# Key and value projections of the first attention as four matmuls at 32-column positions

## Chip, cores, metric

One of the cores of a Trainium2 chip runs the whole kernel. The metric is the device time of one execution in microseconds (us); a lower time is better. Times given "by the profile" are those of one profiled execution.

## What is computed

`x` holds 1024 tokens of 128 features, `ctx_768` 6404 context tokens of 96 features. Four layers follow each other, each an attention of `x` over the context and a feed-forward part, each behind a layer norm and with a residual:

```python
x = x + _L0_xattn_ref(_layernorm(x), ctx_768, ...)   # 16 heads of 8
x = x + _L0_ffn_ref(_layernorm(x), ...)              # 8 experts, top 2
x = x + _L1_xattn_ref(_layernorm(x), ctx_768, ...)   # 16 heads of 64
x = x + _L1_ffn_ref(_layernorm(x), ...)              # fp8 product
x = x + _L2_xattn_ref(_layernorm(x), ctx_768, ...)   # 16 heads of 8
...                                                  # layer 2 experts, layer 3
```

What the change touches belongs to the second attention, `_L1_xattn_ref`, but is worked on inside the first:

```python
k = (context @ Wk).reshape(B, Nk, h, dh)     # Wk, Wv: 96 x 1024, h = 16, dh = 64
v = (context @ Wv).reshape(B, Nk, h, dh)
```

## The kernel before

The program is written by engine, with semaphores set by hand. In the first attention (`attention8(0, 0)`, 16 heads of 8) the heads stand in 4 groups of 4, and each group is worked on for two halves of 512 tokens: 8 passes. A pass goes over the context in 51 tiles (ST) of 128 tokens. For each tile TensorE makes

- the scores, `qk` (L442): four matmuls, each with 32 rows of the array for one head (32 by 128), 512 moving columns, fp32r;
- the attention values, `av` (L454): four matmuls, each with all 128 rows and 32 columns of the array (128 by 32), that write 32 partitions each of one PSUM bank and accumulate over the tiles, fp32.

ScalarE turns the scores into exponentials (L999, two per tile, 128 by 1024), GpSimd stages the tile's keys and values (L1249, L1250). The scores of a tile are issued ahead of the attention values of the tile before it. Scores have six banks, so they wait until an exponential has read the banks that they write.

In between TensorE makes the keys and values of the second attention, since their weights don't depend on `x`. A pass serves one pair of its heads (128 features): `projections1` makes 13 chunks (NC) of up to 512 context tokens for the keys and 13 for the values, 26 jobs (JOBS), the last chunk of each with 384 tokens. JOB_STEPS spreads the jobs over the tiles: in a pass 26 of the 51 tiles have one, between the scores of the next tile and the attention values of this one. All 8 passes together have 208 jobs. A key job (L427) is one matmul with the weights `w[0]` as stationary operand and 512 context columns moving; a value job (L430) is four matmuls (three in the last chunk), each with 128 context tokens as stationary and the 128 columns of `w[1]` moving. Both use the whole 128 by 128 array and write one bank, `ps[:, 7 - half, :]`, which VectorE copies out (L1555, in `move1`) after the semaphore `kv_proj`; a DMA of SyncE's queue then stores the copy to DRAM (L2106). `kv_moved` tells TensorE that the bank is free for the next job. Which of two branches runs is read from data; in this run it is `straight`, in which the tiles are written out one by one. The branch `group`, which also calls `projections1`, is not run.

The two weight matrices `w64` have 128 rows; those beyond the 96 features are part of the contraction as they are, and the change leaves that alone. A matmul of fp32 goes through the array in two passes, and the profile records each with its own weight load: a key job has 2 records of MATMUL and 2 of LDWEIGHTS, a value job 8 and 8, `av` 8 and 8, `qk` (fp32r) 4 and 4.

Of the kernel before, what the change touches and what calls it, by code (L numbers as in the profile page):

```python
# [13 lines left out]
P = 128  # L14
# [20 lines left out]
G = 4  # L35
# [52 lines left out]
def build_program(nc, a):  # L88

    ctx = ExitStack()  # L90
    with ctx:
        def sb(name, shape, dt=F32):
            return ctx.enter_context(nc.sbuf_tensor(name, shape, dt))
# [11 lines left out]
        ctxT = sb("ctxT", [P, NC * HT])  # L105
# [92 lines left out]
        def tok(ap, t):  # L198

            return ap[:, t // 4, (t % 4) * P:(t % 4 + 1) * P]  # L200
# [31 lines left out]
        def _(pe):  # L232
# [93 lines left out]
            for t in range(NT):  # L326
                mm = pe.transpose(ps[:, t // 4, (t % 4) * P:(t % 4 + 1) * P], xn[:, t, :], ident[:, :])
            mm.then_inc(s["turned"], 1)
            for g, (t0, n) in enumerate(VG):
# [6 lines left out]
                for u in range(n):  # L336
                    mm = pe.transpose(ps[0:C, 2 + g % 4, u * P:(u + 1) * P], cn[:, t0 + u, :], ident[:, :])
# [63 lines left out]
            def attention8(n, layer):  # L401
                w = w8[:, n]
# [12 lines left out]
                def projections1(g, half, jobs):  # L415

                    w = [w64[:, 2 * half + m, :] for m in range(2)]
                    bank = ps[:, 7 - half, :]
                    for m, c in jobs:
                        c0, wd = CHUNKS[c]  # L420
                        if m == 0 and c == 0:
                            pe.wait_ge(s["in_wkv"], g * 64 + 32 * half + 32)
                            if half or g is not first_group:
                                pe.wait_ge(s["den_copied"], g * 2 + half + DENS[0])
                        pe.wait_ge(s["kv_moved"], (g * 2 + half) * JOBS + m * NC + c + 1)
                        if m == 0:
                            mm = pe.matmul(bank[:, 0:wd], w[0], ctxT[:, c0:c0 + wd], start=True, stop=True)  # L427
                        else:
                            for u in range(0, wd, P):
                                mm = pe.matmul(bank[:, u:u + P], ctxT[:, c0 + u:c0 + u + P], w[1], start=True, stop=True)  # L430
                        mm.then_inc(s["kv_proj"], 1)

                def queries_ready(g, half):
# [24 lines left out]
                def group(gi, par):  # L458
                    g = gi if n == 0 else gi * 2 + par
                    for half in range(2):  # L460
                        def qk_maxima():
                            queries_ready(g, half)
                            for j in range(G):
                                band = slice(32 * j, 32 * j + 32)
                                mm = pe.matmul(ps[:, j, :], kst[band, 0, :], qh[band, half, :], start=True, stop=True)
                            return mm

                        maxima(layer, g * 2 + half, G, 2 * ST, qk_maxima)
                        def last_sums():
                            if half:  # L470
                                denominators(g * 2, 0)
                            elif n == 0:
                                if g is not first_group:
                                    denominators(g * 2 - 1, 1)
                            elif par:
                                denominators(gi * 4 + 1, 1)
                            else:
                                with pe.If(gi >= 1):
                                    denominators(3, 1)

                        first = (g * 2 + half) * ST + TILES[layer]
                        if n == 0:
                            stream_jobs(first, lambda t, r: qk(half, t, r), lambda *at: av(g, half, *at), last_sums,
                                        lambda step: projections1(g, half, [(step // JSTEPS, c) for c in JOBS_AT[step % JSTEPS]]))
                        else:
                            stream(first, lambda t, r: qk(half, t, r), lambda *at: av(g, half, *at), last_sums)

                def straight():

                    queries_ready(0, 0)  # L490
                    qk(0, TILES[layer], 0)
                    for gh in range(2 * NG):
                        g, half = gh // 2, gh % 2
                        for t in range(ST):
                            at = gh * ST + t + TILES[layer]
                            if t + 1 < ST:
                                qk(half, at + 1, (t + 1) % RING)
                            elif gh + 1 < 2 * NG:
                                queries_ready((gh + 1) // 2, 1 - half)
                                qk(1 - half, at + 1, 0)  # L500
                            if n == 0:
                                projections1(g, half, [divmod(k, NC) for k in range(JOBS) if JOB_STEPS[k] == t - RING])
                            av(g, half, at, t % RING, t == 0, t + 1 == ST)
                            if t == RING - 1 and gh:
                                denominators(gh - 1, 1 - half)
# [16 lines left out]
                for half in range(2):  # L522
                    for g in range(NG):
                        if g == NG - 1:
                            pe.wait_ge(s["o_done"], SUMS[layer] + 2 * g + half + 3)
                        mm = pe.matmul(ps[:, 4 + half, :], w[:, 3 + g, :], sums[:, 2 * g + half, :],
                                       start=(g == 0), stop=(g == NG - 1))
# [58 lines left out]
            for h in range(2):  # L586
                mm = pe.matmul(ps[:, h, :], wT[:, 0, :], z[:, h, :], start=True, stop=True)
            mm.then_inc(s["p_proj"], 1)
            pe.wait_ge(s["p_ready"], 1)
            for t in range(NT):  # L590
                pe.matmul(ps[:, 6, t * E16:t * E16 + E8], tok(t1, t), wT[:, 5, 0:E8], start=True, stop=True)
                mm = pe.matmul(ps[:, 6, t * E16 + E8:t * E16 + E8 + 1], tok(t2, t), ones[:, 0:1], start=True, stop=True)
# [8 lines left out]
            for p in range(NP):  # L601
                cut = slice(p * P, (p + 1) * P)
                mm = pe.matmul(ps[:, 6 + p // 4, (p % 4) * P:(p % 4 + 1) * P], wqk1[0:C, 0, cut], wqk1[0:C, 0, cut],
                               start=True, stop=True)
# [19 lines left out]
            for p in range(NP):  # L624
                if p >= 2:
                    pe.wait_ge(s["b1_copied"], p - 1)
                for h in range(2):
                    mm = pe.matmul(ps[:, 2 * (p % 2) + h, :], wqk1[:, 1, p * P:(p + 1) * P], z[:, h, :], start=True, stop=True)
# [107 lines left out]
            for p in range(NP):  # L736
# [4 lines left out]
                for h in range(2):  # L741
                    mm = pe.matmul(ps[:, h, :], wo8[:, p, :], qo[:, p, h, :], start=(p == 0), stop=(p == last_pair))
# [23 lines left out]
            for t in range(NT):  # L766
                mm = pe.matmul(ps[:, 6, t * E16:t * E16 + E8], tok(z, t), wr2[:, :], start=True, stop=True)
# [3 lines left out]
            for t in range(NT):  # L771
                mm = pe.matmul(ps[:, t // 4, (t % 4) * P:(t % 4 + 1) * P],
                               stat[:, 16 + t:17 + t].to_broadcast([P, P]), ident[:, :], start=True, stop=True)
# [4 lines left out]
            for t in range(ST):  # L778
                k = P if t < SF else TAIL
                mm = pe.matmul(ps[0:C, 2, 0:C], cn2[0:k, t, :], cn2[0:k, t, :], start=(t == 0), stop=(t == ST - 1))  # L780
# [6 lines left out]
            for h in range(2):  # L787
                mm = pe.matmul(ps[:, h, :], wT[:, 1, :], z[:, h, :], start=True, stop=True)
# [3 lines left out]
            for h in range(2):  # L792
                mm = pe.matmul(ps[:, 2 + h, :], wk3[:, :], t1[:, h, :], start=True, stop=True)
# [4 lines left out]
            for h in range(2):  # L798
                mm = pe.matmul(ps[:, 4 + h, :], stat[:, 0:1].to_broadcast([P, P]), z[:, h, :], start=True, stop=True)
# [3 lines left out]
            for g, (t0, m) in enumerate(VG):  # L803
                if g >= 2:
                    pe.wait_ge(s["v3_copied"], g - 1)
                for u in range(m):
                    mm = pe.matmul(ps[:, 6 + g % 2, u * P:(u + 1) * P], ctxT[0:C, (t0 + u) * P:(t0 + u + 1) * P],
                                   wT[0:C, 3, :], start=True, stop=True)
# [22 lines left out]
            for h in range(2):  # L831
                mm = pe.matmul(ps[:, h, :], ones_b[:, :], t2b[:, h, :], start=True, stop=True)
# [8 lines left out]
            for t in range(NT):  # L841
                mm = pe.matmul(ps[:, 0, t:t + 1], tok(t3, t), ones[:, 0:1], start=True, stop=True)
            mm.then_inc(s["den_ready"], 1)
            pe.wait_ge(s["rec_ready"], SUMS[3] + 1)
            for t in range(NT):
                mm = pe.matmul(tok(ps[:, 2:4, :], t), ccol[:, 1, t:t + 1].to_broadcast([P, P]), ident[:, :], start=True, stop=True)
            mm.then_inc(s["den8"], 1)
            pe.wait_ge(s["o_done"], SUMS[3] + 3)
            for h in range(2):
                mm = pe.matmul(ps[:, 2 + h, :], wT[:, 2, :], t1[:, h, :], start=True, stop=True)  # L850
# [5 lines left out]
            for t in range(NT):  # L856
                mm = pe.matmul(ps[:, 6, t * E16:(t + 1) * E16], tok(z, t), wT[:, 4, 0:E16], start=True, stop=True)
# [54 lines left out]
            for t in range(NT):  # L912
                mm = pe.transpose(ps[0:E16, 6 + t // 4, (t % 4) * P:(t % 4 + 1) * P], route[:, 7, t * E16:(t + 1) * E16], ident[:, :])
# [13 lines left out]
            for t in range(NT):  # L927
                mm = pe.transpose(ps[:, t // 4, (t % 4) * P:(t % 4 + 1) * P], tok(xT, t), ident[:, :])
# [1291 lines left out]
```

## Time and profile before

| | us |
|---|---|
| median of 3 runs | 4024.19 |
| their lowest and highest | 4022.65 to 4025.73 |
| profiled execution, its own time | 4020.67 |
| its span, first to last instruction | 4018.9 |
| first attention's eight passes, by the trace | 80.6 to 955.3 |
| TensorE busy | 3690.8 (92% of the span) |
| ScalarE busy | 2595.9 (65%) |
| VectorE busy | 1716.9 (43%) |
| mean granted TensorE clock | 0.979 |

The profile records each engine's instructions with start and modelled or measured end. PE stands for the matmuls, PEld for the weight loads, which can lie beside matmuls; DVE is VectorE, ACT ScalarE, POOL GpSimd, SP SyncE. Matmuls are pipelined, so a record's length is more than the time until the next can start: prices of matmuls are read from start to start. An engine's idle time is put down to what released it.

### The profile page before, as it was taken

How to read it: one execution, taken by the hardware profiler on the slowest of the kernel's cores; microseconds unless marked ns; L12 is line 12 of the kernel's file. 1: busy time of each engine (PE TensorE's matmuls, PEld its weight loads, DVE VectorE, ACT ScalarE, POOL GpSimd, SP SyncE). 2: the span in 40 equal slices, each digit the busy share in tenths (PEclk: the TensorE clock that was granted, in tenths of full speed). 3: DMA queues.
4: the chain of work that ended last, by engine and by line, in shares of the span. 5: the costliest groups of instructions: out<-in, count | busy, mean ns of one | idle time of the engine just before them, and what ended most of it. 6: DMA issues, size and time to landing. Idle time of an engine off the chain costs nothing.

```text
span 4018.9 us, 75707 instructions
## 1 busy us (share of the span) xinstructions
PE 3690.8 (92%) x26700; PEld 1367.5 (34%) x26704; DVE 1716.9 (43%) x1661; ACT 2595.9 (65%) x2756; POOL 464.7 (12%) x1844
## 2 busy tenths in 40 slices
PE   7999999998989999999999999968888888798989
PEld 4333333334533333333333333331111111355444
DVE  4212222223167777777777777640000000443344
ACT  5888888885345555555655555459999999202321
POOL 1222222221000000000000000002222222100210
PEclk8999999999989999999999999989999999899989
DMA  5223222211211111111111110050101000100000
GB/s 175 87 77 92 74 83 81 89 62 45 83 40 38 41 38 37 42 38 36 43 36 38 41 38 5 6 155 3 37 3 37 4 3 1 41 26 1 0 10 29
DMA packets 109842, 182.57 MB, mean 45 GB/s; under 512 B 23700, under 2 KB 46896, under 8 KB 107408
## 3 DMA queue, kind: packets, MB, share of 16 engines
q1 hardware_dynamic: 109584, 178.75, 14.4%
q8 instruction: 209, 3.42, 0.3%
q14 instruction: 49, 0.40, 0.0%
HBM read 107.13 MB, written 71.57 MB: 44 GB/s over the span
## 4 chain that ended last, share of the span: by engine, by line
PE 70%; ACT 15%; issue 10%; DVE 4%; ACTq 1%; SPq 0%; DMA 0%; POOLq 0%; DVEq 0%; POOL 0%
PE ps L657 18%; PE ps L682 17%; ACT probs L999 14%; PE ps L454 6%; PE ps L442 5%; PE ps L561 3%; PE ps L430 3%; PE ps L427 3%; PE ps L540 2%; PE ps L815 2%; PE ps L826 2%; PE ps L874 2%; PE ps L888 1%; PE ps L547 1%; PE ps L256 1%
## 5 line engine op out<-in xcount | busy, mean ns | idle before, releaser
L999 ACT ACTIVATE probs<-ps 128x1024 f32<-128x1024 f32 x1632 | 1520.1, 1085 | 137.2 <-PE ps L442 137.1
L1096 ACT ACTIVATE probs<-ps 128x1024 f32<-128x1024 f32 x816 | 835.8, 1024 | 595.0 <-PE ps L657 580.6
L1728 DVE TENSOR_TENSOR vbuf<-vbuf,probs 128x1024 f32<-128x1024 f32 (+1 forms) x800 | 972.5, 1224 | 333.5 <-ACT probs L1096 333.5
L454 PE MATMUL ps<-probs,vst 128*32 128x512 f32 x6528 | 872.8, 607 | 137.3 <-ACT probs L999 137.0
L442 PE MATMUL ps<-qz,kst 32*128 32x512 f32 x3264 | 415.2, 494 | 57.0 <-ACT probs L999 38.5
L442 PEld LDWEIGHTS ps<-qz,kst 32*128 32x128 f32 x3264 | 167.1, 182 | 748.1 <-issue 555.2
L1555 DVE COPY qs<-ps 128x512 f32<-128x512 f32 (+1 forms) x208 | 141.7, 681 | 647.6 <-PE ps L430 339.3
L1249 POOL CAST kst<-kb 128x128 fp32r x816 | 240.9, 295 | 1373.8 <-PE ps L454 1263.7
L657 PE MATMUL ps<-probs,kb 64*64 64x512 f32 x2560 | 332.3, 589 | 0.0
L1594 DVE COPY work<-ps 128x512 f32 x16 | 11.1, 692 | 702.6 <-PE ps L454 702.6
L657 PE MATMUL ps<-probs,qz 64*64 64x512 f32 x2048 | 268.2, 594 | 6.7 <-issue 6.4
L454 PEld LDWEIGHTS ps<-probs,vst 128*32 128x32 f32 x6528 | 129.1, 108 | 407.7 <-ACT probs L999 328.5
L682 PE MATMUL ps<-probs,qz 64*64 64x512 f32 x2048 | 267.1, 592 | 0.0
L682 PE MATMUL ps<-probs,kb 64*64 64x512 f32 x2048 | 265.8, 589 | 0.0
L1250 POOL COPY vst<-vbuf 128x36 f32 x816 | 177.8, 218 | 0.0
L657 PEld LDWEIGHTS ps<-probs,kb 64*64 64x64 f32 x2560 | 97.9, 133 | 176.7 <-issue 176.7
L1275 POOL COPY probs<-kb 128x512 f32<-128x512 f32 x16 | 14.8, 934 | 1135.3 <-PE ps L657 1080.0
L1017 ACT ACTIVATE probs<-ps,stat 128x1024 f32<-128x1024 f32 x51 | 56.8, 1113 | 123.0 <-PE ps L815 123.0
L682 PE MATMUL ps<-probs,klo 64*64 64x512 f32 x1024 | 132.9, 589 | 0.0
L657 PE MATMUL ps<-probs,klo 64*64 64x512 f32 x1024 | 132.9, 589 | 0.0
L682 PE MATMUL ps<-probs,qs 64*64 64x512 f32 x1024 | 132.9, 589 | 0.0
L540 PE MATMUL ps<-work,vbuf 128*128 128x512 f32 x256 | 121.3, 623 | 9.5 <-DVE probs L1615 8.0
(364 smaller groups left out, 3037.1 us busy)
## 6 DMA issues: line engine op xcount, KB each, us to landing
kv_scratch<-qs SPq DMA_DIRECT2D x192, 256.0 KB, 2.0
kb<-k_scratch SPq DMA_DIRECT2D x24, 816.0 KB, 7.1
kb<-kv_scratch SPq DMA_DIRECT2D x72, 256.0 KB, 2.8
qz<-kv_scratch SPq DMA_DIRECT2D x64, 256.0 KB, 2.9
k_scratch<-klo SPq DMA_DIRECT2D x24, 512.0 KB, 3.3
vbuf<-in_L_ffn_W SPq DMA_DIRECT2D x32, 256.0 KB, 3.1
klo<-kv_scratch SPq DMA_DIRECT2D x32, 256.0 KB, 2.9
qs<-kv_scratch SPq DMA_DIRECT2D x24, 256.0 KB, 3.0
```

Of the source, the lines that this page charges most:

```text
L427: mm = pe.matmul(bank[:, 0:wd], w[0], ctxT[:, c0:c0 + wd], start=True, stop=True)
L442: mm = pe.matmul(ps[:, (4 * r + j) % (2 * RING), :], kst[band, r, :], qh[band, half, :], start=True, stop=True)
L454: mm = pe.matmul(ps[32 * j:32 * j + 32, 6 + half, :], vst[:, r, 32 * j:32 * j + 32], probs[:, r, j * HT:(j + 1) * HT], start=start, stop=stop)
L540: mm = pe.matmul(ps[:, 2 * (f % 2) + h, :], wts[:, f * P:(f + 1) * P], z[:, h, :], start=True, stop=True)
L657: mm = pe.matmul(ps[key, 2 * b + e, :], kk[t // 4][head, (t % 4) * P + HD64 * kh:(t % 4) * P + HD64 * (kh + 1)], qp[head, odd, h, :], star ...
L682: mm = pe.matmul(ps[head, 4 + 2 * h + kh, :], vv[t // 4][key, (t % 4) * P + HD64 * e:(t % 4) * P + HD64 * (e + 1)], pr1[key, (i + 2 * odd) ...
L999: act.activation(probs[:, r, b * T:(b + 1) * T].rearrange("p (h n) -> p h n", h=2), ps[:, 2 * buf:2 * buf + 2, :], ACT.Exp, scale=HD8 ** - ...
L1096: act.activation(pr1[:, (u + 2 * odd) % 4], ps[:, 2 * b:2 * b + 2, :], ACT.Exp, scale=HD64 ** -0.5)\
L1249: pool.tensor_copy(kst[:, r, :], kb[:, par, bass.ds(t * P, P)]).then_inc(s["staged"], 1)
L1250: pool.tensor_copy(vst[:, r, :].rearrange("p (j w) -> p j w", j=G)[:, :, 0:HD8 + 1], vbuf[:, bass.ds(t * (H * (HD8 + 1)) + g * (G * (HD8 + ...
L1555: dve.tensor_copy(kvst[:, slot, 0:wd], ps[:, 7 - half, 0:wd]).then_inc(s["kv_moved"], 1)
L1728: dve.tensor_tensor(sum1[0:k, odd, h], sum1[0:k, odd, h], e, ALU.add).then_inc(s["added"], 1)
```

## The change

Both branches of `projections1` issue each matmul as four, one for each 32 columns of the stationary operand. Matmul `j` writes partitions `32 j` to `32 j + 31` of the same bank: for the keys these are 32 output features of `w[0]`, for the values 32 context tokens. The moving operand is the same for the four. Waits, the semaphore increment on the last matmul, banks and the other engines' programs stay.

```diff
                         if m == 0:
-                            mm = pe.matmul(bank[:, 0:wd], w[0], ctxT[:, c0:c0 + wd], start=True, stop=True)
+                            for j in range(G):
+                                cut = slice(32 * j, 32 * j + 32)
+                                mm = pe.matmul(bank[cut, 0:wd], w[0][:, cut], ctxT[:, c0:c0 + wd], start=True, stop=True)
                         else:
                             for u in range(0, wd, P):
-                                mm = pe.matmul(bank[:, u:u + P], ctxT[:, c0 + u:c0 + u + P], w[1], start=True, stop=True)
+                                for j in range(G):
+                                    cut = slice(32 * j, 32 * j + 32)
+                                    mm = pe.matmul(bank[cut, u:u + P], ctxT[:, c0 + u + 32 * j:c0 + u + 32 * j + 32], w[1],
+                                                   start=True, stop=True)
                         mm.then_inc(s["kv_proj"], 1)
```

## Rows read from the trace of the kernel before

**Rows 1.** The page: busy time of each engine, then the chain that ended last.

```profile
PE 3690.8 (92%) x26700; PEld 1367.5 (34%) x26704; DVE 1716.9 (43%) x1661; ACT 2595.9 (65%) x2756; POOL 464.7 (12%) x1844
...
PE 70%; ACT 15%; issue 10%; DVE 4%; ACTq 1%; SPq 0%; DMA 0%; POOLq 0%; DVEq 0%; POOL 0%
PE ps L657 18%; PE ps L682 17%; ACT probs L999 14%; PE ps L454 6%; PE ps L442 5%; PE ps L561 3%; PE ps L430 3%; PE ps L427 3%; PE ps L540 2%; PE ps L815 2%; PE ps L826 2%; PE ps L874 2%; PE ps L888 1%; PE ps L547 1%; PE ps L256 1%
```

**Rows 2.** Table by stage: two passes of layer 0, one of layer 2; header names columns.

```profile
core 0: us, PE busy (x) PEld busy (x) DVE busy (x) ACT busy (x) POOL busy (x), PEclk, DMA share, GB/s
189.70:299.10 109.40, 103.34 (x742) 34.99 (x742) 23.06 (x30) 96.36 (x103) 23.54 (x102) 1.00 0.22 75
299.10:408.50 109.40, 103.33 (x742) 35.00 (x742) 23.06 (x30) 96.35 (x103) 23.41 (x102) 1.00 0.35 89
...
2774.00:2869.00 95.00, 78.55 (x618) 18.80 (x618) 5.91 (x5) 94.19 (x104) 23.75 (x104) 1.00 0.02 4
```

**Rows 3.** The chain that ended last, 605.72 to 609.95: start us, us, what.

```profile
605.72 0.49 PE ps L442 x4
606.21 1.01 ACT probs L999
607.22 0.14 issue
607.35 0.51 PE ps L442 x4
607.86 1.09 PE ps L430 x8
608.95 0.99 PE ps L454 x8
```

**Rows 4.** Groups by line, six passes, 190 to 846 us: busy, mean ns | idle before.

```profile
L999 ACT ACTIVATE probs<-ps 128x1024 f32<-128x1024 f32 x613 | 579.1, 1031 | 78.3 <-PE ps L442 78.3
...
L1555 DVE COPY qs<-ps 128x512 f32<-128x512 f32 (+1 forms) x156 | 106.3, 681 | 469.9 <-PE ps L430 254.4 <-PE ps L427 215.5
```

**Rows 5.** Timeline of TensorE around one key job: start us, us, what.

```profile
311.28 0.51 PE L442 MATMUL ps<-qz,kst 32*128 32x512 f32 x4
311.71 0.70 PE L427 MATMUL ps<-ctxT,w 128*128 128x512 f32 x1
312.25 0.59 PE L427 MATMUL ps<-ctxT,w 128*128 128x512 f32 x1
312.77 0.64 PE L454 MATMUL ps<-probs,vst 128*32 128x512 f32 x4
313.22 0.61 PE L454 MATMUL ps<-probs,vst 128*32 128x512 f32 x4
313.76 0.50 PE L442 MATMUL ps<-qz,kst 32*128 32x512 f32 x4
```

**Rows 6.** Timeline of TensorE around one value job and the tile after it.

```profile
603.56 0.38 PE L430 MATMUL ps<-w,ctxT 128*128 128x128 f32 x1
...
604.22 0.50 PE L430 MATMUL ps<-w,ctxT 128*128 128x128 f32 x3
604.34 0.39 PE L430 MATMUL ps<-w,ctxT 128*128 128x128 f32 x2
604.65 0.64 PE L454 MATMUL ps<-probs,vst 128*32 128x512 f32 x4
...
605.65 0.51 PE L442 MATMUL ps<-qz,kst 32*128 32x512 f32 x4
606.09 0.64 PE L454 MATMUL ps<-probs,vst 128*32 128x512 f32 x4
```

**Rows 7.** Timeline of the weight loads in the same stretch.

```profile
603.56 0.97 PEld L430 LDWEIGHTS ps<-w,ctxT 128*128 128x128 f32 x8 [0.25 <-issue]
604.65 0.16 PEld L454 LDWEIGHTS ps<-probs,vst 128*32 128x32 f32 x8
```

**Rows 8.** Timeline, second attention: matmuls of one shape in a row, and loads.

```profile
1700.25 1.04 PE L682 MATMUL ps<-probs,work 64*64 64x512 f32 x8
1701.11 1.04 PE L657 MATMUL ps<-probs,qz 64*64 64x512 f32 x8
...
1700.68 0.15 PEld L657 LDWEIGHTS ps<-probs,qz 64*64 64x64 f32 x4 [0.28 <-issue]
```

**Rows 9.** Weight loads of L427, then of L454: ns min/median/max, starts, forms.

```profile
L427 PEld LDWEIGHTS ps<-ctxT,w x208: 186/188/190, 86.9 to 899.8; 128*128 128x128 f32 x104
...
L454 PEld LDWEIGHTS ps<-probs,vst x6528: 105/108/153, 80.7 to 3433.8; 128*32 128x32 f32 x198
```

**Rows 10.** The page: instructions in all, and the queue that fetches them.

```profile
span 4018.9 us, 75707 instructions
...
q8 instruction: 209, 3.42, 0.3%
```

## Prediction, made before the changed kernel had run

> **What bounds the kernel now.** I read the page first [rows 1]: TensorE (PE) is busy for 92% of the span and carries 70% of the chain that ended last, so time taken off PE can be time taken off the end, if it is taken where PE leads. The two edited lines are L427 (key projection) and L430 (value projection), each 3% of that chain. They run only in the eight head-group passes of the first attention, 80.6 to 955.3 us. The table by stage [rows 2] shows what leads there: a pass takes 109.4 us, ScalarE is busy for 96.4 of them, PE for 103.3, and the granted clock is 1.00. The same attention in layer 2, without projections, takes about 95 us per pass with ScalarE busy for almost all of it. So ScalarE sets a floor near 95 to 96, and the projections put some 14 us on top of it in each pass.
>
> The chain of waits in one stretch [rows 3] shows how. Where a tile carries a projection, the chain goes scores (L442), projection, attention values (L454), scores, and only then to an exponential; the whole 1.09 us of the projection stands in it. The lines over six passes [rows 4] say the same from ScalarE's side: it sits idle for 78.3 us before its exponentials, all of it waiting for L442. Six passes hold 156 projection jobs (26 each: 13 chunks, for keys and for values), so each job makes ScalarE wait some 0.50 us. Anything up to that which a job gives back goes straight to the end of the pass; above it ScalarE would hold the pace. VectorE only copies each result out [rows 4], 0.68 us of work in a pass-step of over 2 us, and waits for PE before it.
>
> **The change part by part.** It touches no wait, no semaphore, no DMA and no other engine. One 128x128 stationary load and one matmul become four loads of 32 columns and four matmuls, each writing 32 partitions, with the same moving columns. Every matmul here goes through the array in two passes (the records count two per matmul), so a value job of four token blocks goes from 8 load-and-matmul pairs to 32, a key job from 2 to 8.
>
> First the prices, in the stretch of one key job [rows 5]. From scores to the projection, 311.28 to 311.71, is 0.43 us, and from scores straight to attention values [rows 6], 605.65 to 606.09, is 0.44: leaving the scores' shape costs the same whichever shape follows, so this entry stays. Inside the key job the first pass lasts 0.54 (311.71 to 312.25) although 512 columns stream in 0.43, which the steady stream of L657 and L682 shows (four passes at a time, 0.86 for two [rows 8]). The extra 0.11 is the first load of 128 columns, which nothing hides. The attention values pay the same thing for 32 columns only: 312.77 to 313.22 is 0.45, an extra of 0.02 to 0.03. The load records agree [rows 9]: 188 ns for 128 columns, 108 for 32, a difference of 0.08. The second pass of the key job is followed after 0.52 (312.25 to 312.77), again 0.09 over the 0.43. Attention values to scores shows it too: 313.22 to 313.76 is 0.54, which is 0.43, some 0.02 for the stagger of the four, and 0.09. L657 to L682, which share a shape, shows none of it [rows 8]. So 0.09 is the price of changing the array's shape when full-height (128-row) work is in it, and the edit removes one such change per job, because projection and attention values then have the same shape.
>
> A key job after the edit: 0.03 for the first loads, 0.43 and 0.43 for two rounds of four, 0.89 against 1.06 now. Its attention values then find their first weights loaded behind it, 0.97 against 0.99 to 1.00. Together 0.195 less.
>
> A value job [rows 6]: now 603.56 to 604.65, 1.09, with a pitch of 0.11 between passes of 128 columns (604.22 to 604.34). After: 0.03 and eight rounds at 0.11, 0.91, if four column positions stream at once and the next block's loads hide behind them as they do now. With 0.02 to 0.03 off the attention values, 0.20 less. Eight of the 104 jobs of each kind are shorter ones (384 columns), with the same extras saved.
>
> Sum: 104 x 0.195 + 104 x 0.20 = 41 us. All of it is on the chain, since it is less than the 0.50 that ScalarE waits per job; next late after it is still this wait, at 0.30.
>
> **Unknown costs.** The trace has no column-tiled matmul of 128 moving columns, none whose four positions stream the same columns, and no such density of instructions. The bounds for the value job: below, loads and streaming perfectly overlapped, 0.88 (gain 0.03 more per job, 3 us in all). Above, the four positions run one after another: 32 pairs at the present pitch of 0.11, 3.5 us. I take 0.91, because the nearest row by shape, L454, starts all eight of its loads within a record of 0.16 us while L430's eight take 0.97 [rows 7], and its four matmuls share each round. In [rows 8] the loads of the next group start right behind the last round of the group before on the same positions. Sharing the same moving columns can't gain anything; I price it at zero, with the serial case as its other end. Instruction fetch: a key job gains 6 matmul records, a value job 24 (18 where it is short), and as many loads, some 6,100 records on top of 75,707 [rows 10]. A pass then has about 1,130 matmul records instead of 742 [rows 2], 1.5 times the rate. The instruction queue moves 209 packets for the whole, 362 records to a packet on average, and each takes 0.3% x 16 x 4018.9 / 209 = 0.9 us. No row of now shows PE waiting for one, so I price it at zero; its other end is that every packet of the eight passes shows, (11,860 + 6,140) / 362 = 50 of them, 45 us.
>
> Against the change stands a rule of the Trainium skill, page TensorE: Matmul & The Clock Gate, section Back-to-back issue gap: a stream of weight load and matmul pairs at 128 moving columns was seen to sustain about 81 ns per pair. Taken as a limit for the whole engine, an estimate from that page makes the value job 32 x 0.081 = 2.6 us and the kernel 104 x (2.6 - 1.09) - 20 = 137 us slower. It is the mechanism of the first rival below, which has its price from rows. The eight pairs of L454 in [rows 7] start in far less, but they are a burst and not a stream, so the trace doesn't refute it.
>
> The page TensorEngine Tiling (Array Packing), section Key Properties, says that changing the tiling mode drains the engine; rows show the 0.09, but also that leaving the 32-row scores costs nothing, which the page doesn't distinguish. By the page alone the number of changes falls from three to two a job as well.
>
> **Rivals.** *Pairs are issued too slowly (slower).* Four times as many pairs pass through one sequencer and one queue. The streaming of a value job needs a new pair every 0.11 / 4 = 28 ns. If a pair costs p, the job takes 32p; a value job is worse than now above 1.09 / 32 = 34 ns, and above some 40 ns, (1.09 + 0.20) / 32, it also eats the keys' 20 us. The densest sustained stream in the trace is eight pairs in 0.86 us [rows 8], 107 ns each, and it is paced by its columns, so it bounds nothing tighter; at that price the job takes 3.4 us, 2.35 more, and the kernel 104 x 2.35 - 20 = 224 us slower, 4248. At twice the needed 28 ns it would be 1.8 us, +0.7 each, 53 us slower, 4077. For it: nothing so dense is in the trace. Against: the bursts of [rows 7].
>
> *Values gain nothing, keys do.* The reordering across four positions doesn't reach over to the next token block: each block of 128 columns then pays its first loads and a stagger, 0.05 to 0.08 four times, and the value job ends where it was. Then only the keys' 20 us are left, 4004. Against it: [rows 8].
>
> *The edit doesn't save the change of shape.* The 0.09 might belong to the wait of L454 rather than to the shape. Then 0.08 and 0.02 per job stay, 21 us, 4003. Against: the same 0.09 stands before L442 as well.
>
> *No change.* The saved time is given back by instruction fetch, up to the 45 us above: about 4024.
>
> **How the numbers follow.** The profiled execution took 4020.67 us (span 4018.9); less 41 is 3979.7. The median of the three timed runs, 4024.19, lies 3.5 above it, and less 41 it is 3983. Chances: forecast 0.72 (3977 to 3992); values gain nothing, or the shape change stays, together 0.14 (near 4003); no change 0.05; slower by the issue of pairs 0.09. The range is 3976 to 4005: the forecast, its lower bound of 3 us more with the spread of the runs, and the partial cases, 0.86 together. A measurement of this kernel can tell about 0.2%, 8 us, from no change. Faster 0.86, same 0.05, slower 0.09.
>
> **What would show it.** Right: a pass of 104.2 us instead of 109.4; L454 following the last round of L427 after 0.43, not 0.52; key jobs of 0.89 and value jobs of 0.91 from first start to L454's first; ScalarE's idle before L999 down from 0.50 to 0.30 per job; later stages unchanged. Wrong: value rounds pitched wider than 0.11, loads of L430 that don't start in fours, or gaps in PE at regular numbers of instructions.

## The result

The changed kernel takes 3980.13 us, median of four runs (3977.84 to 3985.2), against 4023.9 for the kernel before, median of four (4022.65 to 4025.73). The ratio is 0.9893, 95% interval 0.9875 to 0.991: 1.1% faster, clear of the 0.2% that can be told from no change. The forecast was 3983. Measured again beside the last of the experiments it took 3982.65 (four runs), ratio 0.9903 (0.9886 to 0.9919).

The page of the changed kernel, and its table by stage for two passes (these rows answer to [rows 1], [rows 2] and [rows 10]; L429 is now the key projection, L434 the value projection, L459 the attention values, L447 the scores, L1004 the exponentials):

```profile
span 3978.8 us, 81851 instructions
PE 3650.2 (92%) x29772; PEld 1357.5 (34%) x29776; DVE 1716.5 (43%) x1661; ACT 2596.5 (65%) x2756; POOL 465.9 (12%) x1844
...
q8 instruction: 233, 3.82, 0.4%
```

```profile
core 0: us, PE busy (x) PEld busy (x) DVE busy (x) ACT busy (x) POOL busy (x), PEclk, DMA share, GB/s
184.20:288.20 104.00, 98.01 (x1130) 33.29 (x1130) 23.03 (x30) 96.32 (x103) 23.70 (x102) 1.00 0.24 80
288.20:392.20 104.00, 98.03 (x1130) 33.32 (x1130) 23.05 (x30) 96.34 (x103) 23.59 (x102) 1.00 0.36 94
```

A pass went from 109.4 to 104.0 us at the same granted clock of 1.00. The whole execution has 6,144 more records and 24 more packets of instructions, 256 records for each packet gained. ScalarE's work in a pass is the same, 96.3; what shrank is its wait. Groups by line of the changed kernel, the same six passes (184.2 to 808.8 us), as in [rows 4]:

```profile
L1004 ACT ACTIVATE probs<-ps 128x1024 f32<-128x1024 f32 x613 | 579.1, 1031 | 46.5 <-PE ps L447 45.5
```

ScalarE's wait for the scores was 78.3 us and is 46.5: 0.30 us for each of the 156 jobs instead of 0.50, as forecast. The timeline of TensorE in the changed kernel, first around a key job (as [rows 5]), then around a value job (as [rows 6] and [rows 7]), columns start us, us, what:

```profile
511.73 0.51 PE L447 MATMUL ps<-qz,kst 32*128 32x512 f32 x4
512.16 0.64 PE L429 MATMUL ps<-ctxT,w 128*32 128x512 f32 x4
512.62 0.61 PE L429 MATMUL ps<-ctxT,w 128*32 128x512 f32 x4
513.05 0.61 PE L459 MATMUL ps<-probs,vst 128*32 128x512 f32 x4
513.48 0.61 PE L459 MATMUL ps<-probs,vst 128*32 128x512 f32 x4
514.02 0.51 PE L447 MATMUL ps<-qz,kst 32*128 32x512 f32 x4
```

```profile
452.05 0.32 PE L434 MATMUL ps<-w,ctxT 128*32 128x128 f32 x4
...
452.62 0.51 PE L434 MATMUL ps<-w,ctxT 128*32 128x128 f32 x12
452.73 0.40 PE L434 MATMUL ps<-w,ctxT 128*32 128x128 f32 x8
452.94 0.61 PE L459 MATMUL ps<-probs,vst 128*32 128x512 f32 x4
453.92 0.51 PE L447 MATMUL ps<-qz,kst 32*128 32x512 f32 x4
...
452.05 0.81 PEld L434 LDWEIGHTS ps<-w,ctxT 128*32 128x32 f32 x32 [0.25 <-issue]
452.84 0.24 PEld L459 LDWEIGHTS ps<-probs,vst 128*32 128x32 f32 x8
```

Read from start to start: the key job is 513.05 - 512.16 = 0.89 (1.06 before), the value job 452.94 - 452.05 = 0.89 (1.09), the attention values 514.02 - 513.05 = 0.97 (0.99). The second round of the key job is followed by L459 after 0.43, not 0.52. The first loads of L459 begin at 452.84, 0.10 before its first matmul: they run while the value job's last round still streams. In [rows 7] the first load of L454 begins only with its matmul, at 604.65. Over all full-size jobs of the trace the medians are 0.882 for keys (1.056 before), 0.897 for values (1.088) and 0.972 behind either (0.996).

### The profile page after: what moved, and what is told of

Read it like the earlier page. It is cut to its first block, busy times and chain, and to the rows that moved or that the text cites. A ratio compares the mean times of both kernels' runs of the same rounds, so it can differ in the third digit from the quotient of the medians.

```text
span 3978.8 us, 81851 instructions
## 1 busy us (share of the span) xinstructions
PE 3650.2 (92%) x29772; PEld 1357.5 (34%) x29776; DVE 1716.5 (43%) x1661; ACT 2596.5 (65%) x2756; POOL 465.9 (12%) x1844
## 4 chain that ended last, share of the span: by engine, by line
PE 69%; ACT 15%; issue 10%; DVE 4%; ACTq 1%; SPq 0%; DMA 0%; POOLq 0%; DVEq 0%; POOL 0%
PE ps L662 18%; PE ps L687 18%; ACT probs L1004 14%; PE ps L459 5%; PE ps L447 5%; PE ps L566 3%; PE ps L434 3%; PE ps L429 3%; PE ps L820 2%; PE ps L545 2%; PE ps L831 2%; PE ps L879 2%; PE ps L893 1%; PE ps L552 1%; PE ps L256 1%
## 5 line engine op out<-in xcount | busy, mean ns | idle before, releaser
L1004 ACT ACTIVATE probs<-ps 128x1024 f32<-128x1024 f32 x1632 | 1520.1, 1085 | 93.9 <-PE ps L447 92.4
L459 PE MATMUL ps<-probs,vst 128*32 128x512 f32 x6528 | 867.0, 603 | 139.3 <-ACT probs L1004 138.5
L447 PE MATMUL ps<-qz,kst 32*128 32x512 f32 x3264 | 413.8, 494 | 55.7 <-ACT probs L1004 37.2
L447 PEld LDWEIGHTS ps<-qz,kst 32*128 32x128 f32 x3264 | 166.4, 182 | 745.9 <-issue 553.8
L459 PEld LDWEIGHTS ps<-probs,vst 128*32 128x32 f32 x6528 | 148.6, 108 | 380.1 <-ACT probs L1004 326.8
```

What stands on the lines that cost most here:

```text
L447: mm = pe.matmul(ps[:, (4 * r + j) % (2 * RING), :], kst[band, r, :], qh[band, half, :], start=True, stop=True)
L459: mm = pe.matmul(ps[32 * j:32 * j + 32, 6 + half, :], vst[:, r, 32 * j:32 * j + 32], probs[:, r, j * HT:(j + 1) * HT], start=start, stop=stop)
L1004: act.activation(probs[:, r, b * T:(b + 1) * T].rearrange("p (h n) -> p h n", h=2), ps[:, 2 * buf:2 * buf + 2, :], ACT.Exp, scale=HD8 ** - ...
```

## Experiments

The forecast left two questions. Which part of the job's price went, and is it the change of shape or any narrower load? And how near were the rivals, those on the issue of pairs (a weight load and its matmul) above all? A third came up with the numbers: ScalarE still waited 0.30 us per job, and it did so in lumps, since 26 tiles of a pass carry a whole job and the others none.

### Keys alone, values alone

```diff
 # keys: only L429 is four matmuls; values: only L434
-mm = pe.matmul(bank[:, 0:wd], w[0], ctxT[:, c0:c0 + wd], ...)
+for j in range(G):
+    mm = pe.matmul(bank[cut, 0:wd], w[0][:, cut], ctxT[:, c0:c0 + wd], ...)
```

> Only the key projection is issued as four 32-column matmuls; the value projection stays one 128x128 matmul per block. Theory A (each job loses one change of the array's shape, 0.09 us, 0.08 us of the first weight load, and 0.024 us of the first load of the attention values behind it): key job 0.88 us from its first start to L454's first (1.056 before), value job 1.088 as before, attention values 0.972 behind a key job and 0.996 behind a value job; kernel 104 x 0.198 = 20.6 us faster than before, 4003. Theory B (only the shorter loads count, the 0.09 belongs to L454's own wait): key job 0.97, kernel 11 us faster. Theory C (the gain comes mostly from the value job's denser streaming): under 10 us faster.

Measured: 4000.29 us, ratio 0.995 (0.9933 to 0.9966), a pass of 106.8 us.

> Only the value projection is issued as four 32-column matmuls per block. Theory A: value job 0.897 us against 1.088, its attention values 0.972, key job 1.056; kernel 104 x 0.215 = 22.4 us faster than before, 4001.5; with the run on the keys it adds up to the change. Theory B: value job 0.99, 12 us faster. Theory C: 33 us or more.

Measured: 3998.0 us, ratio 0.9938 (0.9918 to 0.9959), a pass of 106.6 us. The tables by stage, one pass of each, keys first:

```profile
292.60:399.40 106.80, 100.77 (x820) 34.52 (x821) 23.03 (x31) 96.33 (x103) 23.59 (x102) 1.00 0.36 92
```

```profile
291.40:398.00 106.60, 100.57 (x1052) 33.78 (x1052) 23.08 (x31) 96.39 (x103) 23.41 (x102) 1.00 0.36 92
```

2.6 us and 2.8 us of a pass, 5.4 together: the whole change. In the trace of the first the key job is 0.882, the value job 1.088, and attention values 0.972 or 0.996 by which job is ahead of them; in the second it is the other way round. The two halves add up and neither touches the other. The intervals of the gains are 13.7 to 27.0 us for the keys and 16.5 to 33.0 for the values. The expected 20.6 and 22.4 us lie inside them, theory B's 11 and 12 and theory C's under 10 for the keys outside; C's 33 for the values stands at the edge, and the pass (8 x 2.8 = 22 us) is against it.

### Columns of 64: tiled, but another shape than the attention values

```diff
-for j in range(G):
-    cut = slice(32 * j, 32 * j + 32)
+for j in range(2):
+    cut = slice(64 * j, 64 * j + 64)
```

> Both projections as two matmuls of 64 columns at 64-column positions: column-tiled, but not the shape of the attention values (32 columns), so the change of shape between projection and L454 stays. Theory A: only the first load shrinks, from 128 to 64 columns, 0.053 us; key job 1.00 us, value job 1.03, L454 to L442 still 0.996; kernel 208 x 0.053 = 11 us faster than before, 4013. Rival (any column tiling does it, whatever its width): the 0.09 and the 0.024 go too, key job 0.91, 208 x 0.17 = 35 us faster, 3988.

Measured: 4009.46 us, ratio 0.9968 (0.9955 to 0.998), a pass of 108 us. The timeline of TensorE around one key job and one value job of it:

```profile
657.18 1.08 PE L429 MATMUL ps<-ctxT,w 128*64 128x512 f32 x4
658.19 1.06 PE L459 MATMUL ps<-probs,vst 128*32 128x512 f32 x8
659.19 0.51 PE L447 MATMUL ps<-qz,kst 32*128 32x512 f32 x4
```

```profile
695.12 1.09 PE L434 MATMUL ps<-w,ctxT 128*64 128x128 f32 x16
696.14 1.07 PE L459 MATMUL ps<-probs,vst 128*32 128x512 f32 x8
697.14 0.51 PE L447 MATMUL ps<-qz,kst 32*128 32x512 f32 x4
```

The key job is 1.01, the value job 1.02, and the attention values 1.00: the whole price of the change of shape is back, and only the shorter first load and, for the values, a little of the pitch between rounds are saved. The rival, 0.17 per job for any tiling, falls: its 3988 us lies below the lowest of the six runs, 4006. So of the change's 0.17 for a key job some 0.08 are the first load (128 columns down to 32, 0.03 per 32 columns, as [rows 9] had it) and 0.09 the shape, and the shape must be that of the work behind. Over all full-size key jobs the sum closes for three widths: two rounds of 0.427 and a first load of 0.107, 0.053 or 0.027 for 128, 64 or 32 columns, with 0.095 where L454's shape differs, give 1.056, 1.00 and 0.881; the medians are 1.056, 1.009 and 0.882.

### The same pairs, one position after another

```diff
-for u in range(0, wd, P):
-    for j in range(G):
+for j in range(G):
+    for u in range(0, wd, P):
```

> The change, but the value projection's loops are swapped: all token blocks at one column position, then the next position. The same 32 load-and-matmul pairs in another order. Theory D (pairs leave the queue in order; one at a position that is still busy holds back those behind it, so neighbours in program order must stand at different positions): the blocks of a position go one after another, 8 passes of 0.107 each, and the positions overlap only at their ends, value job 3 us or more, kernel 200 us slower than the change. Rival E (the engine picks freely among some 64 queued instructions): 16 instructions for each position fit, the four positions run side by side, value job near 0.9 us, kernel as the change.

Measured: 4120.76 us in one run, a pass of 121.2 us, 140 us slower than the change. The timeline of TensorE around one value job:

```profile
657.27 2.13 PE L434 MATMUL ps<-w,ctxT 128*32 128x128 f32 x29
659.13 0.63 PE L459 MATMUL ps<-probs,vst 128*32 128x512 f32 x3
659.24 0.49 PE L434 MATMUL ps<-w,ctxT 128*32 128x128 f32 x3
659.56 1.02 PE L459 MATMUL ps<-probs,vst 128*32 128x512 f32 x5
660.52 0.51 PE L447 MATMUL ps<-qz,kst 32*128 32x512 f32 x4
```

From the first start to the next scores it is 3.25 us, where the change has 1.87, for the same 32 pairs. Neither theory had the size: D, with 3 us or more for the job and 200 us for the kernel, was nearer than E, with no loss. In the single records the first position runs its eight passes 0.11 apart, and the second position starts 0.467 after the first, when the first starts its fifth pass: three pairs of it are still ahead. The third and fourth follow at 0.93 and 1.40. So the engine does look past work that waits for a busy position, which D denied, but only by about three pairs here; the attention values even begin (659.13) before the last three passes of the value job, at positions that are free. The order of the loops in the change, position innermost, needs no more than this and gets the full overlap.

### More and smaller pairs: how near was the rival

```diff
 for u in range(0, wd, P):
+    for v in range(0, P, 64):        # or 32
         for j in range(G):
-            mm = pe.matmul(bank[cut, u:u + P], ..., w[1], ...)
+            mm = pe.matmul(bank[cut, u + v:u + v + 64], ..., w[1][:, v:v + 64], ...)
```

> The change, with each value matmul cut into two of 64 moving columns: 64 load-and-matmul pairs per value job instead of 32, the same columns in all. This asks how near the issue of pairs is to being the bound (the rival on the slower side). A round of four positions streams in 0.053 us, so a pair is needed every 13 ns. If pairs can be issued at the 6.6 ns at which four positions start one behind another, the job stays near 0.90 to 0.95 us and the kernel within 5 us of the change; if the floor is p per pair the job takes 64 p, so with 25 ns 1.6 us and the kernel 73 us slower than the change.

Measured: 3983.1 us in one run. Timeline of TensorE:

```profile
557.50 1.10 PE L435 MATMUL ps<-w,ctxT 128*32 128x64 f32 x64
558.42 1.04 PE L460 MATMUL ps<-probs,vst 128*32 128x512 f32 x8
```

64 pairs in 0.92 us, 14 ns each, twice as dense as the change needs. The rival on the slower side is ruled out. The Trainium skill, page TensorE: Matmul & The Clock Gate, section Back-to-back issue gap, gives some 81 ns per pair at 128 moving columns; as a limit for the whole engine that does not hold here. For a single position no run tests it: pairs of 128 columns came 0.11 us apart at one position in the order above, as on the whole array in the kernel before, so they were never as dense as that figure.

> The same cut into four of 32 moving columns: 128 pairs per value job, a round streams in 0.027 us, a pair is needed every 6.7 ns, and each load of 32 columns (0.027 us) is as long as the stream that hides it. With a floor p per pair above 6.7 ns the job takes 128 p: at 10 ns 1.3 us and 40 us slower than the change, at 25 ns 3.2 us and 240 us slower. It also fetches some 18,000 more records; if fetching were a limit, gaps in the trace would show up that don't belong to a job.

Measured: 4131.5 us in one run, 151 us slower than the change, passes from 119 to 128 us. Two stretches of the timeline of TensorE, a value job without and one with a gap:

```profile
562.60 1.27 PE L435 MATMUL ps<-w,ctxT 128*32 128x32 f32 x126
563.68 0.60 PE L460 MATMUL ps<-probs,vst 128*32 128x512 f32 x1
...
564.69 0.50 PE L448 MATMUL ps<-qz,kst 32*128 32x512 f32 x4
```

```profile
415.67 0.98 PE L435 MATMUL ps<-w,ctxT 128*32 128x32 f32 x91
422.63 0.70 PE L435 MATMUL ps<-w,ctxT 128*32 128x32 f32 x35 [5.98 <-issue]
```

Where no gap falls, the job takes 563.68 - 562.60 = 1.08 us, 8.5 ns a pair: still no floor of 10. That costs 0.19 x 104 = 20 us. The rest is gaps like the second, in which TensorE waits for nothing that another engine does; there are some 50 of over 1 us in the eight passes. In the stretches of value jobs the queue of instructions then fetches a packet every 4.0 us in the median (by its records; most take 1.0 to 1.3 us), where the change has 7.7 and the cut into 64 has 5.2, with one such gap. The records tie the gaps to the packets: of the 50, all but one end 1.2 to 1.6 us after a packet of that queue has landed, a stretch of time in which only one in seven of the value job's matmuls starts. So instruction fetch is the likely cause. It was not isolated, by a run that keeps the density and changes the fetching alone, and the size of this case's limit stays open.

### The lumps: half a job in each tile

```diff
+HALF_STEPS = [k - sum(k > d for d in (0, 12, 26, 38)) for k in range(2 * JOBS)]
...
+lo, hi = (0, wd) if not part else ((0, 2 * P), (2 * P, wd))[part[0]]
+# columns lo:hi of the chunk; kv_moved is waited for where lo == 0, kv_proj told where hi == wd
...
-projections1(g, half, [divmod(k, NC) for k in range(JOBS) if JOB_STEPS[k] == t - RING])
+projections1(g, half, [(*divmod(k // 2, NC), k % 2) for k in range(2 * JOBS) if HALF_STEPS[k] == t - RING])
```

> The change, with each job cut into two halves (256 of its 512 context columns) that stand in successive tiles, so that 44 of a pass's tiles carry half a job (0.45 us) and four carry a whole one, instead of 26 tiles with a whole one. Theory F (ScalarE's wait comes from the lumps, not from the amount: per tile PE needs 0.437 + 0.45 + 0.972 = 1.86 us and ScalarE's two exponentials 1.88): the pass falls from 104.2 to 96 to 98 us, ScalarE never waits for long, kernel 50 to 65 us faster than the change, about 3925. Rival (the jobs cost their full PE time on the end wherever they stand): the pass stays at 104 us, 3980.

Measured: 3959.06 us, ratio to before 0.9842 (0.9825 to 0.9858), 21 us faster than the change; a pass of 102 us (one 104), not 96 to 98. The rival, 104 us for every arrangement, falls, but the gain is less than half of the expected 50 to 65 us, and ScalarE's wait over six passes only went from 46.5 to 40.9. Timeline of TensorE and VectorE at the start of a pass:

```profile
493.79 3.35 DVE L1540 RECIPROCAL qs<-qs 128x512 f32<-128x512 f32 x1
493.85 1.07 PE L432 MATMUL ps<-ctxT,w 128*32 128x256 f32 x16 [0.74 <-issue]
...
497.17 0.69 DVE L1543 TENSOR_TENSOR work<-work,qs 128x512 f32<-128x512 f32 x1
497.78 0.68 DVE L1564 COPY qs<-ps 128x512 f32<-128x512 f32 x1
498.52 1.08 PE L432 MATMUL ps<-ctxT,w 128*32 128x256 f32 x8 [2.31 <-DVE qs L1564]
```

The first job's copy stands on VectorE behind the reciprocal of the previous pass's denominators (3.35 us), so the second job, now one tile later, waits 2.3 us for its bank. In the kernel before and in the change the second job comes three tiles after the first; this arrangement had closed that distance up.

> The kernel before (128x128 jobs), cut into halves in the same way. A half then pays the first load and the change of shape itself: 0.107 + 0.427 + 0.095 = 0.63 us, PE needs 0.437 + 0.63 + 0.996 = 2.06 us per tile, above ScalarE's 1.88. Theory A with F: a pass of about 44 x 2.06 plus four at 2.49 plus three at 1.88 = 106 us, kernel 25 to 30 us faster than before, 3995, and the shape of the matmuls is worth 65 to 75 us between the two kernels with halves instead of 44. If the shape change were not a price of its own, the two would lie under 45 us apart.

Measured: 4029.49 us, ratio to before 1.0019 (1.0009 to 1.0029), no gain where 25 to 30 us were expected. Most passes take 110 to 111 us (one 114) instead of 106; the expectation did not have the wait just shown. The two kernels with halves share that wait and lie 70 us apart, inside the expected 65 to 75. A half at 128x128 takes 0.63 (a tile's period in the trace: 2.07), a half at 32 columns 0.46 (1.87).

With steps 1 and 2 of a pass left free:

```diff
-HALF_STEPS = [k - sum(k > d for d in (0, 12, 26, 38)) for k in range(2 * JOBS)]
+HALF_STEPS = [0, 0] + [k + 1 - sum(k > d for d in (10, 20, 30, 40, 50)) for k in range(2, 2 * JOBS)]
```

> The halves again, but no job in the first tiles of a pass after the first whole one (steps 1 and 2 free), and five tiles instead of four that carry a whole job. In the halves before, TensorE waited 2.3 us in each pass for VectorE's copy of the first job, which stood behind the reciprocals of the previous pass, and ScalarE up to 3.8 us for it; a pass took 102 instead of the expected 96 to 98. If that is the cause, a pass is now 51 x 1.87 + 5 x 0.44 + 1.1 for the denominators' matmul = 98.6 us, and the kernel 8 x (104.0 - 98.6) = 43 us faster than the change, 3937. If the lumps weren't what ScalarE waited for, the pass stays at 102 us or more.

Measured: 3932.08 us (3931.66 to 3934.84), ratio to before 0.978 (0.9764 to 0.9796), 51 us faster than the change on the same chip (3982.65). Timeline and table by stage:

```profile
519.67 0.50 PE L451 MATMUL ps<-qz,kst 32*128 32x512 f32 x4
520.11 0.64 PE L432 MATMUL ps<-ctxT,w 128*32 128x256 f32 x8
520.56 1.04 PE L463 MATMUL ps<-probs,vst 128*32 128x512 f32 x8
521.54 0.51 PE L451 MATMUL ps<-qz,kst 32*128 32x512 f32 x4
```

```profile
275.50:373.90 98.40, 96.71 (x1234) 36.00 (x1230) 23.05 (x30) 95.19 (x103) 23.56 (x102) 1.00 0.39 100
```

A pass takes 98.4 us, as worked out (98.6), with TensorE and ScalarE both busy for nearly all of it. The sum had counted five tiles with a whole job; with the first there are six, which by the same sum would be 99.1. ScalarE's wait over six passes is down to 19.7 us, from 46.5. This version beats both kernels. The 128x128 halves were not run with the two steps free, so what they would gain in this arrangement is not shown.

## Why the prediction was right, point by point

- *What bounds the kernel.* Right: all that a job gave back reached the end of the pass, and ScalarE's wait fell from 0.50 to 0.30 per job. Seven passes went from 109.1 to 109.5 down to 103.9 to 104.0, one to 104.5. At the end of the eighth, at the copy of its denominators, the kernel is 41.7 us ahead (954.5 to 912.8 us), and 1.6 us of that are lost in later stages, which no step named and which is of the size of the spread between runs.
- *Key job.* 0.89 forecast, 0.882 measured. The 0.09 for the change of shape, the weakest step since rows of before showed it only as a remainder, is borne out by the 64-column run.
- *Value job.* 0.91 forecast, 0.897 measured. The round has a pitch of 0.109, a little under the 0.11 taken. Sharing the same moving columns between four positions costs nothing that can be seen.
- *Attention values.* 0.02 to 0.03 off, 0.024 measured.
- *Sum.* 104 x (0.198 + 0.215) = 43 us by the medians against the 41 forecast; the profiled span fell by 40.1, the medians of the runs by 43.8. The forecast of 3983 had added 3.5 us because the median of the runs before lay that far above the profiled one; in the changed kernel it does not (3980.13 and 3980.54).
- *Instruction fetch.* Priced at zero, with 45 us as the other end. The price is borne out: no gap of over 0.3 us lies inside a value job of the change. The one pass of 104.5 waits longer ahead of its first key job (1.36 us after the scores, where that pass had 1.05 before and the others have 0.89); why is not shown. The other end was too low: the growth was 24 packets, one for 256 records, where 362 to a packet had made it 17, so the eight passes have 72 packets and not 50, and at 0.9 us each they would be 65 us.
- *The rival of slow issue* had 0.09. The cut into 64 columns shows 14 ns a pair, half the 28 needed, so the margin was at least a factor of two, and of three with the cut into 32. The argument against it was weaker than it was put: in [rows 7] only the loads of L454 start in a burst, while its matmuls come four at a time, 0.45 us apart [rows 5]. *Values gain nothing* fell with the values alone; *the shape isn't saved* with 64 columns.
- *Next late is still this wait, at 0.30.* Right. That it came from lumps and could be spread was not seen in the prediction; on top of the change it was worth another 51 us, more than the change itself.

## What to carry to other kernels

Where small matmuls stand ahead of a group that uses the array in another shape, give them the shape of that group: here 0.09 us of switching and 0.03 us per 32 columns of the first load came back each time, though the instructions are four times as many. Write the positions innermost, since the engine here looked only about three pairs past a busy one. Then see who waits for the lumps: half a job in each tile gained another 51 us, once VectorE's copy of the first job had room. The cheaper halves make a tile of 1.87 us on TensorE, just under ScalarE's 1.88; the 128x128 halves make 2.07 and gained nothing as they were run.

## What the runs showed of the hardware

- Leaving the 32-row shape of the scores costs nothing, whichever shape follows (0.43 to 0.44 us in every kernel where no other wait falls there); leaving work of 128 rows for another shape costs 0.09 us. The Trainium skill, page TensorEngine Tiling (Array Packing), section Key Properties, has every switch of the tiling mode drain the engine. The trace shows a price on one side only.
- Four positions took 64 pairs in 0.92 us and 128 in 1.08 us, 14 and 8.5 ns per pair of weight load and matmul.
- A pair that waits for its position let about three pairs of the same position be passed over, and no more: the same 32 pairs took 1.87 us to the next scores in one order and 3.25 in the other.
- At 128 pairs per value job gaps of 1 to 6 us appeared that no engine's wait explains, with instruction packets some 4 us apart; 49 of 50 ended 1.2 to 1.6 us after a packet had landed.
